# One score visit per unit in place of two, and QKV two units ahead, in an attention and expert layer

## What is computed

```python
xn = _layernorm(x, axis=-1)
# attention, per batch
q, k, v = split(xn @ wqkv.T); q, k, v = heads(q), heads(k), heads(v)     # 16 heads of 64
q = _rope(_rmsnorm(q, q_norm_w), cos, sin); k = _rope(_rmsnorm(k, k_norm_w), cos, sin)
attn = softmax(where(causal, q @ k.T * 64 ** -0.5, -inf)); a = (attn @ v) @ wo.T
# experts, per row
chosen = argmax(xn @ gate_w.T); e = xn + expert_w[chosen] @ xn
x = x + a + e
```

## Time and profile before

| what | value |
|---|---|
| runs | 2035.03 us median of three (2033.85 to 2035.99) |
| profiled execution | its own span is 2031.8 us; what lies around it is not in the profile, and comes to 3.2 us against the median |
| TensorE clock granted | full in all of forty slices but the first (0.8) |
| DMA | 145.81 MB, 72 GB/s over the span |

### The profile page before, as it was taken

The page is one execution under the profiler, slowest core; times in us unless marked ns, Lnnn a source line. Parts: engine busy times, 40 slices in busy tenths (PEclk is TensorE's granted clock), DMA queues, the critical chain, the costliest instruction groups (busy, mean ns, idle before and its releaser), DMA issues.

```text
span 2031.8 us, 48319 instructions
## 1 busy us (share of the span) xinstructions
PE 1966.0 (97%) x16520; PEld 1640.7 (81%) x16520; DVE 1740.2 (86%) x4144; ACT 1604.4 (79%) x5095; POOL 1374.6 (68%) x1975
## 2 busy tenths in 40 slices
PE   4899999999999999999999999999999999999997
PEld 4777888888888888888888888888888888888885
DVE  5799888888888898888988889889888898888875
ACT  3887887888788788787878878878878887888775
POOL 6667766577666767658766686666876677765764
PEclk8999999999999999999999999999999999999999
DMA  5111211112211132112221122221222112222244
GB/s 188 58 51 37 68 49 63 58 45 79 94 56 48 48 100 79 57 54 60 74 92 48 48 81 71 74 64 53 64 74 84 48 53 84 69 69 63 83 131 149
DMA packets 84548, 145.81 MB, mean 72 GB/s; under 512 B 9808, under 2 KB 63184, under 8 KB 84176
## 3 DMA queue, kind: packets, MB, share of 16 engines
q1 hardware_dynamic: 78160, 125.93, 19.5%
q0 software_dynamic: 6144, 16.79, 2.5%
HBM read 102.05 MB, written 40.63 MB: 70 GB/s over the span
## 4 chain that ended last, share of the span: by engine, by line
PE 80%; POOL 8%; DVE 6%; ACT 3%; issue 2%; DMA 1%; POOLq 0%; DVEq 0%
PE ps_g L737 35%; PE ps_g L834 14%; PE ps_g L843 11%; PE ps_s L823 10%; PE ps_g L799 5%; POOL rms_inv L526 3%; PE ps_s L816 3%; POOL qk_rot L520 3%; POOL qk_rot L531 2%; DVE qk_sin L1015 1%; PE ps_g L764 1%; DVE qk_cos L1015 1%; ACT prob L618 1%; PE ps_g L746 1%; ACT qk_sq L602 1%
## 5 line engine op out<-in xcount | busy, mean ns | idle before, releaser
L520 POOL TENSOR_TENSOR qk_rot<-qk_cos,qk_sin 128x128 f32<-128x128 f32 x1024 | 464.9, 475 | 577.3 <-DVE qk_sin L1015 571.2
L737 PE MATMUL ps_g<-w_qkv,xn_t 128*128 128x384 f32 (+1 forms) x3072 | 639.6, 351 | 2.3 <-DVE xn_t L930 1.5
L618 ACT ACTIVATE prob<-ps_s,neg_max 128x256 f32<-128x256 f32 (+3 forms) x1024 | 534.9, 548 | 0.3 <-DVE neg_max L1029 0.3
L737 PEld LDWEIGHTS ps_g<-w_qkv,xn_t 128*128 128x128 f32 x3072 | 526.2, 190 | 5.5 <-issue 2.2
L526 POOL TENSOR_TENSOR rms_inv<-ss,neg_half 128x8 f32<-128x8 f32 x256 | 448.0, 1750 | 0.0
L1029 DVE TENSOR_REDUCE neg_max<-ps_s 128x2 f32<-128x512 f32 (+3 forms) x512 | 404.7, 809 | 0.8 <-PE ps_s L823 0.8
L628 ACT ACTIVATE prob_t<-ps_g 128x512 f32<-128x512 f32 (+2 forms) x768 | 369.0, 526 | 37.9 <-PE ps_g L834 37.9
L834 PE MATMUL ps_g<-ident,prob 128*128 128x128 f32 x2560 | 360.7, 278 | 3.9 <-DVE prob L1040 1.6
L834 PEld LDWEIGHTS ps_g<-ident,prob 128*128 128x128 f32 x2560 | 289.9, 140 | 73.5 <-DVE prob L1040 45.1
L531 POOL TENSOR_TENSOR qk_rot<-qk_rot,rms_inv 128x256 f32<-128x256 f32 x512 | 323.5, 652 | 20.1
L843 PE MATMUL ps_g<-prob_t,v 128*64 128x512 f32 (+3 forms) x2048 | 305.6, 441 | 1.0 <-ACT prob_t L628 1.0
(11 more groups left out here) (108 smaller groups left out, 2513.6 us busy)
## 6 DMA issues: line engine op xcount, KB each, us to landing
w_tile<-w_dram SPq DMA_DIRECT2D x120, 512.0 KB, 3.5
x_rows_s<-x_dram SPq DMA_DIRECT2D x120, 128.0 KB, 2.1
y_dram<-y_rows_s SPq DMA_DIRECT2D x120, 128.0 KB, 1.7
xin<-in_x SPq DMA_DIRECT2D x16, 512.0 KB, 4.2
out<-acc SPq DMA_DIRECT2D x15, 512.0 KB, 3.4
w_dram<-w_tile SPq DMA_DIRECT2D x8, 512.0 KB, 2.9
x_dram<-xn SPq DMA_DIRECT2D x2, 1920.0 KB, 18.4
y_back<-in_expert_t SPq DMA_DIRECT2D x8, 256.0 KB, 3.7
```

The lines of the kernel that those rows point to most:

```text
L520: r = pool.tensor_tensor(rot[:, :, a, :], cos[:, :, a, :], sin[:, :, 1 - a, :], ALU.add)
L618: r = act.activation(prob[:, h, prob_at(k):prob_at(k) + w], ps_s[n % 2][:, h, 0:w], ACT.Exp, bias=neg_max[:, i, h:h + 1], scale=1.0, accum ...
L737: r = pe.matmul(ps, lhs(a, c), rhs(b, c), start=(c == parts[0] and (a, b) == TERMS[0]), stop=(c == parts[-1] and (a, b) == TERMS[-1]))
```

## The change

One visit `scores(u)` in place of two. Item 0 gets a bank of the rotating four (`"s"`, the first use of each unit), which both its heads share; item 1 keeps `ps_s[0]`; items 2 and 3 share `ps_s[1]`. The 512-wide terms are cut in two of 256, so that the two heads never write the shared bank at once: in a pair one matmul writes the shared bank and the other another bank, and PE waits on its own semaphore `s_shared_bank` where the shared bank goes from one head to the other, once among the masks and once among the terms. Two items that share a bank are read by DVE and ACT only when both are ready. All four QKV tiles are done two units ahead. The transposes of the probabilities of items 0, 1 and 2 move into the unit itself, item 3 stays behind the next unit's scores. The experts (but the first of several) come behind the projection. The orders of ACT, DVE and POOL follow; semaphores become one per item.

```diff
+        def score_ps(u, k):
+
+            if k == 0:
+                return ps_g[g_bank(u, "s")][:, :].rearrange("p (h w) -> p h w", h=HEADS_OF_PAIR)
+            at = 3 * P if k == 3 else 0
+            return ps_s[k // 2][:, :, at:at + width(k)]
...
             def unit(u):
                 if live(u + 1):
-                    if u >= 0:
-
-                        pool.wait_ge(s_qk_t, 2 * (u + 1))
-                    rotate(u + 1, 0)
-                    rotate(u + 1, 1)
-                    scale(u + 1, (0, 1))
                     rotate(u + 1, 2)
                     rotate(u + 1, 3)
                     scale(u + 1, (2, 3)).then_inc(s_scaled, 1)
...
+                if live(u + 2):
+                    if live(u + 1):
+
+                        pool.wait_ge(s_qk_t, 2 * (u + 2))
+                    rotate(u + 2, 0)
+                    rotate(u + 2, 1)
+                    scale(u + 2, (0, 1))
...
+                if u >= 3:
+                    act.wait_ge(s_o, u - 2)
                 act.activation(v[:, u % 3, t, :], ps[:, 2 * PW:3 * PW], ACT.Copy).then_inc(s_v, 1)
...
+                for half in range(2):
+                    r = mask(0, 0, half, half == 0)
+                    mask(1, 1, half, half == 0)
+                r.then_inc(s_shared_bank, 1)
+                for half in range(2):
+                    mask(0, 1, half, half == 0)
+                    mask(1, 2, half, half == 0)
+                for half in range(2):
+                    mask(0, 2, half, half == 0)
+                    mask(1, 3, half, False)
+                pe.wait_ge(s_shared_bank, 2 * u + 1)
+                for half in range(2):
+                    mask(0, 3, half, False)
+                    mask(1, 0, half, False)
+                for m in range(3):
+                    term(0, 1, m, 0, 2 * P)
+                    r = term(1, 0, m, 0, 2 * P)
+                r.then_inc(s_shared_bank, 1)
+                for m in range(3):
+                    term(0, 1, m, 2 * P, 4 * P)
+                    term(1, 1, m, 0, 2 * P)
+                pe.wait_ge(s_shared_bank, 2 * u + 2)
+                for m in range(3):
+                    last = term(0, 0, m, 0, 2 * P), term(1, 1, m, 2 * P, 4 * P)
...
```

More of the change, by code:

```diff
@@ L293, in pt_count @@
         def pt_count(u, k, part):
-            return sum(len(pt_parts(n)) for n in range(NT)) * u + sum(len(pt_parts(n)) for n in range(k)) + part + 1
+            return len(pt_parts(k)) * u + part + 1
         @lru_cache(None)
@@ L623, in take_pt @@
+                r.then_inc(s_prob[k], 1)
+            def take_pt(u, k, part):
                 i, w = ITEMS[k], width(k)
[L624 to L631, removed]
+                h0, h1 = pt_parts(k)[part]
+                act.wait_ge(s_pt[k], pt_count(u, k, part))
+                act.activation(prob_t[:, h0:h1, 0:i + 1, tile(i)],
+                               ps_g[pt_bank(u, k, part)][:, 0:(h1 - h0) * w].rearrange("p (h j q) -> p h j q", h=h1 - h0, q=P),
+                               ACT.Copy).then_inc(s_prob_t[k], 1)
@@ L664, in unit @@
             def unit(u):
[L665 removed]
+                now = tiles_now(u)
                 if live(u - 1):
[L667 to L672, removed]
+                    take_pt(u - 1, 2, 1)
+                    scale_probs(u - 1, 3)
                 if live(u):
                     softmax(u, 0)
[L675 removed]
+                if live(u - 1):
+                    take_pt(u - 1, 3, 0)
+                if turns_x(u):
+                    for i in sorted_tiles(u):
+                        take_xs(u, i)
+                    take_xt(batch_of(u) + 1)
+                if live(u):
+                    softmax(u, 1)
+                for i in sorted_tiles(u)[0:2] if not turns_x(u) else ():
+                    take_xs(u, i)
+                if live(u):
+                    softmax(u, 3)
+                if u == -1:
+                    high_weights(2)
+                    high_weights(3)
+                if live(u + 2) and not turns_x(u):
+                    take_qkv(u + 2, 0)
                 if live(u - 1):
                     take_o(u - 1)
[L678 to L681 removed]
+                if turns_x(u):
+                    take_qkv(u + 2, 0)
+                for i in now[0:1] if now[1:] else ():
                     take_ys(u, i)
[L683 removed]
+                for i in now[2:3]:
                     take_xs(u, i)
@@ new lines, in transpose_probs @@
+            def transpose_probs(u, k, part):
+                h0, h1 = pt_parts(k)[part]
+                pe.wait_ge(s_scaled_prob[k], u + 1)
+                ps = bank(pt_bank(u, k, part), (s_prob_t[k], pt_count(u, k, part)))
+                for h in range(h0, h1):
+                    for j in range(ITEMS[k] + 1):
+                        r = pe.transpose(ps[:, tile((h - h0) * (ITEMS[k] + 1) + j)],
+                                         prob[:, h, prob_at(k) + j * P:prob_at(k) + (j + 1) * P], ident[:, :])
+                r.then_inc(s_pt[k], 1)
@@ L1060, in unit @@
             def unit(u):
-                tiles = sorted_tiles(u)
+                now = tiles_now(u)
+                if live(u + 1):
+                    rope_products(u + 1, 3)
                 if live(u):
```

309 lines of the change are left out of this document (158 added, 151 removed).

## The result

The changed kernel takes 2061.22 us (median of 4 runs, 2060.55 to 2062.29) against 2035.33 us before: ratio 1.0127, 95% interval 1.0113 to 1.0141. It is 26 us slower, where 15 us less was forecast.

The account below looks back on a forecast made before the run. PE's issue order alone was taken to set the steady time, with DVE's side work hidden. The terms -47 + 18 - 12 - 18 - 4 + 1 + 42 + 5 = -15 us gave 2020 us, range 1982 to 2052.

Parts of the forecast that it names:

- DVE's order: DVE from row maxima to the two products before PE's projection: 1.2 us spare, jobs beyond it delay PE, +42 us.
- All QKV two units ahead: POOL gets its last input at the unit's start, rotating q and k some 6 us before PE turns them: -18 us.
- One visit less: PE's scores: one entry, late first term, late first mask and exit go, 0.37 us per unit, -47 us.
- Own waits: PE's two waits on its own matmuls at the shared bank: 0.12 us at masks, 0.02 at terms, +18 us.
- Transposes of the probabilities: PE's eight transposes behind the first visit: some 0.1 us of wait per unit goes, -12 us.
- DVE's jobs: Extra jobs (statistics, normalising, choice, slots, row start) make PE wait at the projection: +42 us.
- Waits for POOL's q and k: PE's waits for rotated q and k go, the first long one at the start aside: -18 us, -10 to -26.
- The start: The one long wait at the start gains by tiles that lie before it: -4 us, 0 to -13.
- The head of every unit: First masks wait for DVE's products on the third QKV tile, in the shared bank: +5 us, 0 to +38.
- The rivals: Unit heads wait (21%, 2053); shared-bank waits drain the array (8%, 2053); weight loads show (4%, 2065); jobs don't reach PE (15%, 1978).
- Theory A: Experiments' theory of the loss: PE waits at the projection for DVE, whose jobs now stand ahead of the products.
- C: Experiments' theory of the loss: the queues of ACT and POOL cost the gain.

Follow-up runs that it names:

- POOL behind: The changed kernel with POOL's two multiplications of tiles 2 and 3 waiting until DVE's first scaling is done: 2026.13 us.
- needless multiplications: The kernel with POOL behind plus two POOL multiplications into an unread tile, where the real ones had stood: 2060.38 us.
- units of 17.01: Units with ranks in the kernel with POOL behind, DVE's jobs split in halves (choice mostly late) and the weights' splitting moved: 1998.33 us.

## Why the prediction was wrong

The step that failed is the one under "DVE's order": "the reciprocal and scaling (1.01, 1028.70 to 1029.71)". That row came from a unit in which POOL began its multiplication only behind the scaling:

```profile
1029.92 1.18 POOL L531 TENSOR_TENSOR qk_rot<-qk_rot,rms_inv 128x256 f32<-128x256 f32 x2
```

Under "All QKV two units ahead" POOL's earlier input was counted as a gain alone; where its multiplications would then stand was not asked. In the changed kernel they stand at 5.3 us into the unit: beside the scaling where there is no job, and in units with a job beside the job. There a normalising instruction takes 0.72 us in place of 0.41, the first one-hot instruction of a choice 0.52 in place of 0.22, and one step of the slots 0.54 in place of 0.23 (unit 88). A row start is not longer itself (1.21 us), but holds POOL up, which then meets the work behind it. Price, from the kernel with POOL behind and the one with needless multiplications: 35 us. A second term of the same sum was too small: the reciprocal waits 0.44 us for ACT and the first product 0.18 for v, so that even with scalings of 0.88 us the second product ends 0.34 us before the projection (1316.76 to 1317.10), where the forecast had 1.2 us to spare.

The warning stood in the trace of before, in a unit with statistics where POOL's multiplication met the scaling (DVE, then POOL):

```profile
1336.61 1.24 DVE L1040 TENSOR_SCALAR prob<-prob,sum_inv 128x512 f32<-128x512 f32 x2
...
1336.86 1.46 POOL L531 TENSOR_TENSOR qk_rot<-qk_rot,rms_inv 128x256 f32<-128x256 f32 x2
```

1.24 us where the undisturbed pair takes 0.88; the old order hid it from PE, and the unit took 15.13 us. It was no exception: of the old kernel's 256 scalings of 512 columns 37 took 0.84 us and the others 0.48 to 0.49, and of the 256 of 384 columns, which met POOL's rotation (L520), 129 took 0.50 to 0.93 and the others 0.40 to 0.43. The change took it off the narrower ones (2 in place of 129) and put it on the wider ones (103 in place of 37), ahead of PE's projection. The view of this line mixes the two widths, with 401, 486 and 930 ns as minimum, median and maximum: the median hides it, a maximum near twice the median was the sign. The view of waits had a sign too, which the prediction passed over when it named the wait for POOL's q and k as the one that adds up: weight loads waited longer in all for this very line, 0.36 us at a time, though PE itself waited only 1.6 us for it.

```profile
PEld ps_g L834 <- DVE prob L1040: 45.1, 120, 1.9
```

With the 35 us taken out, 2026 is measured where 2020 was forecast. Units 8 to 119 save 7.5 us (1711.3 against 1718.8), where the terms of the sum for all units (-47 + 18 - 12 - 18 + 42 + 5 = -12) give 10.5 for these 112 of 128. That it comes so near is in part luck: PE's own waits and the head of a unit cost some 18 us less than forecast, and the visit, the waits for POOL and the start gave less. Point by point:

- *One visit less*: 0.36 forecast without its masks, 0.33 measured.
- *Own waits*: 0.14 forecast, 0.04 at the masks and nothing visible at the terms: 5 us in place of 18.
- *Transposes of the probabilities*: 0.1 forecast. No run shows the term by itself; of the 0.39 us that units without a job save with POOL behind, 0.33 for the visit less 0.04 for the masks leave 0.10.
- *DVE's jobs*: 42 us forecast. With POOL behind, the units with a job are longer than 14.75 by 0.14 (row start), 0.99 (statistics), twice 0.29 (normalising), 1.39 and 1.05 (choice with and without ranks), 0.88 (slots) and 1.24 (tiles and row start): 6.3 us in 16 units, 44 in units 8 to 119. The mechanism is right and the size near, though 0.33 of the 1.39 were there before (15.47 against 15.14 at place 7).
- *Waits for POOL's q and k*: -18 forecast. Behind the first one PE itself waited 21 us in the old kernel, some 9 in units 0 to 7 and 12 in units 8 to 119, there above all at places 1, 9 and 12 (0.43 to 0.48 each). They are gone. Places 1 and 9 had been 0.65 and 0.69 us longer than 15.14, some 9 us in units 8 to 119; place 12 is no shorter (14.66 with POOL behind). So the term was too large there, and for units 0 to 7, where more changed, its size stays open.
- *The start*: -4 forecast, and +0.5 to +1 measured. Unit 2 starts 6 us earlier (66.86 against 72.90), but unit 8 starts 0.5 us later (164.10 against 163.61). The splitting of the weights, unnamed in the forecast, stands at the end of units 0 to 7 in DVE's new order, ahead of the next unit's products and row maxima. With POOL behind unit 8 starts at 164.55. Moving the splitting was worth 15.6 us.
- *The head of every unit*: 5 us forecast. The changed kernel's waits show none at the first mask but 0.6 us in the last unit; elsewhere it was long only where a late job made it (0.61 us in units of 17.01).
- *The rivals*: the two that would have given 2053 and the one at 2065 are near the measured time, and none of them is its cause.

Theory A is true, but was in the forecast already. What made the miss is part of C, though not by the order of queues: C expected POOL behind the scaling to be slower. What stays open is why, in the changed kernel, the last group's head unit (number 120) took 18.7 us against 16.2; it is 17.2 with POOL behind.

## What to carry to other kernels

When a change moves work to another time on an engine that is not the bound, look at what it will run beside, not only at who waits for it. Take the duration of an instruction from rows with the neighbour that it will have, and read minimum and maximum of a line as well as its median. An order that sets an engine's products on the way of the bound engine turns every job in front of them into lost time: cut such jobs to fit the idle times that the timeline shows (0.4 us ahead of the scaling, 1.1 us ahead of the copy of k), and recheck what comes next.

## What the runs showed of the hardware

- *DVE beside POOL*: DVE's multiplication by a scalar from SBUF to SBUF, 128x512, takes 0.48 to 0.49 us alone and up to 0.84 beside POOL's multiplication of two SBUF operands; POOL's pair takes 1.36 us in place of 1.19. DVE's statistics, its products out of PSUM and its sums of squares (0.41 each) do not change. The two take turns, as the four instructions of unit 83 show one by one:

```profile
1334.56 0.61 POOL L547 TENSOR_TENSOR qk_rot<-qk_rot,rms_inv 128x256 f32<-128x256 f32 x1
1334.70 0.75 DVE L1107 TENSOR_SCALAR prob<-prob,sum_inv 128x512 f32<-128x512 f32 x1
1335.13 0.79 POOL L547 TENSOR_TENSOR qk_rot<-qk_rot,rms_inv 128x256 f32<-128x256 f32 x1
1335.38 0.83 DVE L1107 TENSOR_SCALAR prob<-prob,sum_inv 128x512 f32<-128x512 f32 x1
```

Of the changed kernel's 256 scalings of 512 columns, 97 started while such a multiplication ran, and 96 of these ended 0.28 to 0.29 us after it, wherever in it they had started (the other one, which started 0.15 before its end, 0.33 after). The other way round, all 48 multiplications that started while a scaling ran ended 0.47 us after it. The Trainium skill has such a rule ("SBUF — State Buffer", SBUF: two separate sides): GpSimd shares one pair of SBUF ports with those VectorE instructions that run in a two-port mode or have two SBUF inputs, as a lock held for a whole instruction. The trace agrees, in which instructions collide and in that the second gets on when the first is done. The four took 0.61 + 0.28 + 0.47 + 0.28 = 1.64 us together (1334.56 to 1336.20) and not 0.88 + 1.19 = 2.07, since what lies ahead of the last 0.28 us (DVE) or 0.47 us (POOL) of an instruction ran beside the other.

- *One-hot rows*: a 128x8 instruction of DVE takes 0.22 us. In 14 units of the changed kernel the first of the four met POOL's multiplication; it took 0.50 to 0.54 us and ended 0.03 after it. Four of them took 0.91 us in unit 87 and 1.49 in the late choice, where three met POOL's rotation of q and k (1359.33 to 1361.04).
- *Leaving and entering the 64-row scores* costs PE 0.33 us per visit, with weight loads hidden throughout: 256-wide pairs, with a load ahead of each matmul, follow each other every 0.12 us.
